# Starting the deferred normalisation of an attention group two key steps later, in a differential-attention layer on eight cores

## Chip, cores and metric

One Trainium2 chip, all 8 cores. Every core runs the same program on its own data. The metric is the device time in microseconds of the slowest core; "before" is the median of two runs.

## What is computed

One pre-norm transformer layer on x of shape (4, 4096, 1024): differential attention, then a gated two-expert feed-forward part. The change lies in the attention. Cut to what matters:

```python
# 16 heads, each with two score maps of depth 32 and values of width 64
scores = einsum('bhqd,bhkd->bhqk', q, k)            # 32 maps, s = 4096
probs  = softmax(scores, axis=-1).reshape(b, 16, 2, s, s)
w      = probs[:, :, 0] - lam * probs[:, :, 1]
attn   = einsum('bhqk,bhkd->bhqd', w, v)
rms    = rsqrt(mean(attn * attn, axis=-1) + 1e-5)
attn   = attn * rms * subln_g * (1 - LAMBDA_INIT)
```

Each core takes one batch element and half of its queries (2048), against all 4096 keys.

## The kernel before

The program has three parts: projections into SBUF (Kfm, Qfm, Vtm), the attention, and the output projection with the feed-forward part. Instructions are listed by hand per engine; each engine runs its list in order, and semaphores tie the lists together.

The attention is a loop over 64 groups (16 heads times 4 blocks of 512 queries, `n` at L650). Within a group the loop at L659 takes 32 key tiles of 128, `j`, called steps here. A step has:

- on TensorE (PE), L665 and L670: scores of tile j for the two maps, 32 rows deep, into psS (two halves, taken in turn);
- on PE, for tile j - 1, L678 and L683 (values, 64 columns each, into psA) and L688 and L692 (a matrix of ones, which gives the softmax sums, into psZ); they wait for the exponentials of tile j - 1;
- on ScalarE (ACT), L700: the exponentials of tile j, psS to pt, 128x1024.

L708 to L720 do the value and sum products of the last tile, behind the loop.

What is left of a group, its combine (`make_combine`, L593), is done during the next group. It is a list of 11 thunks:

- s1, VectorE (DVE), L599: reciprocal of psZ, 128x512; it waits until the group's last sum product is done
- s2, DVE, L603: psA times that, into tbuf
- s3, PE, L607: tbuf through Lmat (128x64, fp32), which forms the difference with lambda, into psZ
- s4 and s5, DVE, L611 and L615: copy to abuf, square to sqf
- s6, PE, L619: sqf through ones (64x64, fp32), the sum of squares, into psZ
- s7, DVE, L623: scale and epsilon; after it the psZ and psA of this group are free, which the group after next waits for in its first step (L663)
- s8 and s9, ACT, L629 and L633: Ln and Exp, which give the reciprocal root
- s10, DVE, L638: the scaled result to anbuf
- s11, POOL, L643 (issued in the helper at L108): DMA of anbuf to DRAM

Each fp32 product appears as two matmul instructions in the trace. Lines L704 and L705 put one thunk behind L700 of every even step from j = 4 on, so s1 stands at step 4, s3 at 8, s6 at 14, s8 at 18, s9 at 20 and s11 at 24. That a thunk stands at a step fixes its place in its own engine's list, and nothing else. What is left behind the loop would be issued at L724; the last group's combine is issued whole behind all groups (L727).

Of the kernel before, what the change touches and what calls it, by code (L numbers as in the profile page):

```python
# [63 lines left out]
def build_program(upto="full"):  # L64
# [46 lines left out]
    def T(fn, waits=(), inc=s_pe):  # L111
        return prog.op("tensor", fn, waits, inc)
# [4 lines left out]
    def A(fn, waits=(), inc=s_act):  # L117
        return prog.op("scalar", fn, waits, inc)
# [530 lines left out]
    pending = []  # L649
    for n in range(NGRP):  # L650
# [6 lines left out]
        if n >= 1:  # L657
            pending = make_combine(n - 1)
        for j in range(NT):  # L659
            p = j % 2  # L660
            waits = [(s_se, grp_exp_base + j - 1)]
            if j == 0:
                waits.append((s_dve, max(combine_free[n - 2], c_setup_done)))  # L663
                waits.append((s_act, c_p2_act))
            T(lambda t, p=p, r0=r0, g=g, j=j, qc=qc: t.matmul(  # L665
                psS[:, p * 1024: p * 1024 + 512],
                Kfm[r0:r0 + 32, g * S + j * 128: g * S + (j + 1) * 128],
                Qfm[r0:r0 + 32, g * QT + qc * 512: g * QT + (qc + 1) * 512],
                start=True, stop=True, tile_position=(r0, 0)), waits=waits)
            smm = T(lambda t, p=p, r1=r1, g=g, j=j, qc=qc: t.matmul(  # L670
                psS[:, p * 1024 + 512: p * 1024 + 1024],
                Kfm[r1:r1 + 32, g * S + j * 128: g * S + (j + 1) * 128],
                Qfm[r1:r1 + 32, g * QT + qc * 512: g * QT + (qc + 1) * 512],
                start=True, stop=True, tile_position=(r1, 0)), inc=s_smm)
            if j >= 1:
                jj = j - 1
                pm = jj % 2
                T(lambda t, jj=jj, pm=pm, d=d, aset=aset: t.matmul(  # L678
                    psA[aset][0:64, :], Vtm[:, jj * D + d * 64: jj * D + d * 64 + 64],
                    pt[:, pm * 1024: pm * 1024 + 512],  # L680
                    start=(jj == 0), stop=False, tile_position=(0, 0)),
                    waits=[(s_se, grp_exp_base + jj + 1)])
                T(lambda t, jj=jj, pm=pm, d=d, aset=aset: t.matmul(  # L683
                    psA[aset][64:128, :], Vtm[:, jj * D + d * 64: jj * D + d * 64 + 64],
                    pt[:, pm * 1024 + 512: pm * 1024 + 1024],
                    start=(jj == 0), stop=False, tile_position=(0, 64),
                    skip_group_check=True))
                T(lambda t, jj=jj, pm=pm, aset=aset: t.matmul(  # L688
                    psZ[aset][0:64, :], ones64b[:, :],
                    pt[:, pm * 1024: pm * 1024 + 512],  # L690
                    start=(jj == 0), stop=False, tile_position=(0, 0)))
                prog.op("tensor", lambda t, jj=jj, pm=pm, aset=aset: t.matmul(  # L692
                    psZ[aset][64:128, :], ones64b[:, :],
                    pt[:, pm * 1024 + 512: pm * 1024 + 1024],
                    start=(jj == 0), stop=False, tile_position=(0, 64),
                    skip_group_check=True), inc=s_satt)
            wexp = [(s_smm, smm)]
            if j >= 2:
                wexp.append((s_satt, s_satt.count - 1))
            A(lambda sc, p=p: sc.activation(pt[:, p * 1024: p * 1024 + 1024],  # L700
                                            psS[:, p * 1024: p * 1024 + 1024],
                                            AF.Exp, bias=mneg_bc[:, 0:1], scale=float(SCALE)),
              waits=wexp, inc=s_se)
            if pending and j >= 4 and (j % 2 == 0):  # L704
                pending.pop(0)()  # L705
        jj = NT - 1
        pm = jj % 2
# [454 lines left out]
```

How the kernel before makes its waits and increments, by code:

```python
    def replay(self, eng_obj, name):  # L54
        for ws, fn, inc, incn in self.items[name]:
            for (s, v) in ws:
                eng_obj.wait_ge(s.handle, v)
            instr = fn(eng_obj)
            if inc is not None:
                assert instr is not None, f"op on {name} must return an instruction"
                instr.then_inc(inc.handle, incn)
```

## Time and profile before

| | us |
|---|---|
| time, median of 2 runs | 4235.14 (4234.46 to 4235.81) |
| the profiled execution's own time | 4229.77 |
| its span (slowest core, core 7) | 4228.2 |
| spans of the other seven cores | 4182.9 to 4191.0 |
| PE busy (matmuls) | 3147.4, 74% |
| ACT busy | 2591.6, 61% |
| DVE busy | 1095.7, 26% |
| PE weight loads | 930.1, 22% |

Times below are microseconds from the start of the span unless they say ns. A row that names a line, an engine and an operation is one group of instructions; the arrow reads "out from in". "PEclk" is the share of TensorE's full clock that was granted in a stretch: 1.00 is 2.4 GHz, 0.50 is 1.2 GHz. An engine can be "busy" and still slow.

### The profile page before, as it was taken

The numbers are of one execution on the slowest core, as the hardware profiler recorded it, in microseconds if no ns is written. First come the engines' busy times: TensorE is split into PE (matmuls) and PEld (weight loads), VectorE is DVE, ScalarE is ACT, GpSimd is POOL, SyncE is SP. The second block draws the span as 40 slices with busy tenths as digits, with TensorE's granted clock in tenths as the row PEclk, the third lists the DMA queues.
The fourth block names the chain that finished last, engine by engine and source line by source line (L and its number), as shares of the span: only waits on it lengthen the run. The fifth ranks groups of instructions, "written<-read, shape, count | busy, mean of one in ns | idle before, by whom it ended". The sixth has DMA issues, their size and how long they took to land.

```text
span 4228.2 us, 48628 instructions; the slowest of 8 cores (4182.9 to 4228.2 us)
## 1 busy us (share of the span) xinstructions
PE 3147.4 (74%) x16100; PEld 930.1 (22%) x16100; DVE 1095.7 (26%) x2159; ACT 2591.6 (61%) x3590; POOL 71.1 (2%) x116
## 2 busy tenths in 40 slices
PE   2626637888788888888888878888888888715598
PEld 1313312222222222222222222111221222103332
DVE  3747735211111111111111111111111111116622
ACT  1424511478778778787787777777787777602211
POOL 0001100000000000000000000000000000000000
PEclk9868979789889889898898998776897788757799
DMA  2234421000000000000000000000000000023201
GB/s 82 77 105 119 122 74 45 18 2 2 3 2 3 2 2 3 2 3 2 2 3 2 2 3 2 2 2 2 2 3 2 2 2 3 2 84 93 65 35 45
DMA packets 96042, 108.20 MB, mean 26 GB/s; under 512 B 57780, under 2 KB 70198, under 8 KB 95800
## 3 DMA queue, kind: packets, MB, share of 16 engines
q1 hardware_dynamic: 88888, 84.11, 7.1%
q0 software_dynamic: 6912, 20.98, 1.7%
q8 instruction: 137, 2.24, 0.2%
q14 instruction: 105, 0.86, 0.1%
HBM read 84.09 MB, written 20.97 MB: 25 GB/s over the span
## 4 chain that ended last, share of the span: by engine, by line
PE 48%; ACT 25%; DMA 13%; issue 8%; DVE 4%; ACTq 1%; DVEq 0%; SPq 0%; POOL 0%; POOLq 0%
ACT pt L700 23%; PE psA L678 12%; PE psS L665 11%; PE psZ L688 8%; PE pp L292 4%; PE psE L1049 3%; PE psZ L607 2%; PE psE L1054 2%; DMA xbuf<-x 2%; PE psZ L619 2%; DMA stab<-sink 1%; PE psXO L855 1%; DMA ctab<-cosk 1%; DMA wst<-wo 1%; DMA xbuf<-xq 1%
## 5 line engine op out<-in xcount | busy, mean ns | idle before, releaser
L700 ACT ACTIVATE pt<-psS,mneg_bc 128x1024 bf16<-128x1024 f32 x2048 | 2198.6, 1110 | 642.8 <-PE psS L670 637.8
L678 PE MATMUL psA<-pt,Vtm 128*64 128x512 bf16 x1984 | 883.2, 445 | 456.0 <-ACT pt L700 419.3
L683 PE MATMUL psA<-pt,Vtm 128*64 128x512 bf16 x1984 | 921.4, 464 | 0.0
L692 PE MATMUL psZ<-pt,ones64b_s 128*64 128x512 bf16 x1984 | 885.8, 446 | 0.0
L688 PE MATMUL psZ<-pt,ones64b_s 128*64 128x512 bf16 x1984 | 883.2, 445 | 0.0
L665 PE MATMUL psS<-Qfm,Kfm 32*128 32x512 bf16 x2048 | 881.2, 435 | 1.2 <-DVE Lmat L561 1.2
L670 PE MATMUL psS<-Qfm,Kfm 32*128 32x512 bf16 x2048 | 881.8, 436 | 0.0
L678 PEld LDWEIGHTS psA<-pt,Vtm 128*64 128x64 bf16 x1984 | 221.5, 112 | 1076.7 <-issue 1076.7
L599 DVE RECIPROCAL zrbuf<-psZ 128x512 f32<-128x512 f32 x64 | 214.9, 3358 | 892.9 <-PE psZ L720 892.9
L665 PEld LDWEIGHTS psS<-Qfm,Kfm 32*128 32x128 bf16 x2048 | 184.4, 92 | 1097.4 <-issue 1097.4
L292 PE MATMUL pp<-wbuf,hfmb 128*128 128x512 bf16 x1280 | 334.8, 422 | 81.8 <-DMA hfmb<-hfm_s 42.2
L692 PEld LDWEIGHTS psZ<-pt,ones64b_s 128*64 128x64 bf16 x1984 | 239.3, 121 | 0.0
L688 PEld LDWEIGHTS psZ<-pt,ones64b_s 128*64 128x64 bf16 x1984 | 234.5, 118 | 0.0
L683 PEld LDWEIGHTS psA<-pt,Vtm 128*64 128x64 bf16 x1984 | 221.4, 112 | 0.0
L611 DVE COPY abuf<-psZ 64x512 f32<-64x512 f32 x64 | 43.7, 683 | 662.9 <-PE psZ L607 662.9
L292 PEld LDWEIGHTS pp<-wbuf,hfmb 128*128 128x128 bf16 x1280 | 130.2, 106 | 264.1 <-issue 158.5
L670 PEld LDWEIGHTS psS<-Qfm,Kfm 32*128 32x128 bf16 x2048 | 185.0, 93 | 0.0
L638 DVE TENSOR_TENSOR anbuf<-abuf,rstdb 64x512 bf16<-64x512 f32 x64 | 43.8, 684 | 474.0 <-ACT rstdb L633 474.0
L623 DVE TENSOR_SCALAR ubuf<-psZ 64x512 f32<-64x512 f32 x64 | 43.7, 683 | 428.9 <-PE psZ L619 428.9
L301 ACT CAST qef<-pp 128x512 bf16<-128x512 f32 x48 | 28.1, 585 | 185.5 <-DVE ropeo L314 180.1
L508 ACT CAST Vtm<-pp 128x512 bf16<-128x512 f32 x32 | 18.7, 585 | 192.7 <-PE pp L292 187.8
L855 PE MATMUL psXO<-wo_b,atile 128*128 128x512 bf16 x256 | 83.2, 497 | 70.3 <-DMA atile<-attn_s 70.0
(144 smaller groups left out, 2219.8 us busy)
## 6 DMA issues: line engine op xcount, KB each, us to landing
xbuf<-x SPq DMA_DIRECT2D x32, 512.0 KB
xbuf<-xq SPq DMA_DIRECT2D x16, 512.0 KB
hfm_s<-hfmb POOLq DMA_DIRECT2D x32, 256.0 KB, 3.2
hfmb<-hfm_s SPq DMA_DIRECT2D x32, 256.0 KB
xqb<-xq SPq DMA_DIRECT2D x16, 512.0 KB
wst<-w SPq DMA_DIRECT2D x32, 256.0 KB
out<-ybuf POOLq DMA_DIRECT2D x16, 512.0 KB, 3.0
ctab<-cosk SPq DMA_DIRECT2D x32, 128.0 KB
```

The costliest lines, as they stand in the source:

```text
L292: last = T(lambda t, n=n, c=c: t.matmul(pp[ppb][:, n * 512:(n + 1) * 512], hfm_tile[:, c * 128:(c + 1) * 128], wmat_b[:, c * D + n * 512: ...
L599: st["c1"] = V(lambda v: v.reciprocal(zrbuf[:, :], psZ[bset][:, :]), waits=[(s_satt, (m + 1) * NT)])
L607: st["c4"] = T(lambda t: t.matmul(psZ[bset][0:64, :], Lmat[:, :], tbuf[:, :], start=True, stop=True), waits=[(s_dve, st["c2"])])
L665: T(lambda t, p=p, r0=r0, g=g, j=j, qc=qc: t.matmul(psS[:, p * 1024: p * 1024 + 512], Kfm[r0:r0 + 32, g * S + j * 128: g * S + (j + 1) * 128],
L670: smm = T(lambda t, p=p, r1=r1, g=g, j=j, qc=qc: t.matmul(psS[:, p * 1024 + 512: p * 1024 + 1024], Kfm[r1:r1 + 32, g * S + j * 128: g * S ...
L678: T(lambda t, jj=jj, pm=pm, d=d, aset=aset: t.matmul(psA[aset][0:64, :], Vtm[:, jj * D + d * 64: jj * D + d * 64 + 64], pt[:, pm * 1024: p ...
L683: T(lambda t, jj=jj, pm=pm, d=d, aset=aset: t.matmul(psA[aset][64:128, :], Vtm[:, jj * D + d * 64: jj * D + d * 64 + 64], pt[:, pm * 1024 ...
L688: T(lambda t, jj=jj, pm=pm, aset=aset: t.matmul(psZ[aset][0:64, :], ones64b[:, :], pt[:, pm * 1024: pm * 1024 + 512], start=(jj == 0), sto ...
L692: prog.op("tensor", lambda t, jj=jj, pm=pm, aset=aset: t.matmul(psZ[aset][64:128, :], ones64b[:, :], pt[:, pm * 1024 + 512: pm * 1024 + 1024],
L700: A(lambda sc, p=p: sc.activation(pt[:, p * 1024: p * 1024 + 1024], psS[:, p * 1024: p * 1024 + 1024], AF.Exp, bias=mneg_bc[:, 0:1], scale ...
L855: mm = T(lambda t_, n=n, c=c, ab=ab: t_.matmul(psXO[:, n * 512:(n + 1) * 512], atile[ab][:, c * 128:(c + 1) * 128], wo_b[:, c * D + n * 51 ...
L1049: mm = T(lambda t_, n=n, c=c, t=t, wT=wT, e=e: t_.matmul(psE[e][:, n * 512:(n + 1) * 512], h2_all[:, t * D + c * 128: t * D + (c + 1) * 12 ...
```

## The change

The first step at which a thunk may be placed is 6 instead of 4. The thunks, their order, their waits and their number stay; s1 now stands at step 6, s3 at 10, s6 at 16, s8 at 20, s9 at 22 and s11 at 26.

```diff
@@ -701,7 +701,7 @@
                                             psS[:, p * 1024: p * 1024 + 1024],
                                             AF.Exp, bias=mneg_bc[:, 0:1], scale=float(SCALE)),
               waits=wexp, inc=s_se)
-            if pending and j >= 4 and (j % 2 == 0):
+            if pending and j >= 6 and (j % 2 == 0):
                 pending.pop(0)()
         jj = NT - 1
         pm = jj % 2
```

## Rows read from the trace of the kernel before

**Rows 1.** The page's costliest groups: busy us, mean ns, idle before and releaser.

```profile
L700 ACT ACTIVATE pt<-psS,mneg_bc 128x1024 bf16<-128x1024 f32 x2048 | 2198.6, 1110 | 642.8 <-PE psS L670 637.8
L678 PE MATMUL psA<-pt,Vtm 128*64 128x512 bf16 x1984 | 883.2, 445 | 456.0 <-ACT pt L700 419.3
```

**Rows 2.** The list of cores: span and mean granted clock.

```profile
core 0: 4183.5 us, clock 0.857
...
core 7: 4228.2 us, clock 0.838
```

**Rows 3.** Timeline of ACT, core 7: start, duration, instruction, idle before.

```profile
1520.45 1.11 ACT L700 ACTIVATE pt<-psS,mneg_bc 128x1024 bf16<-128x1024 f32 x1 [0.42 <-PE psS L670]
1521.98 1.11 ACT L700 ACTIVATE pt<-psS,mneg_bc 128x1024 bf16<-128x1024 f32 x1 [0.42 <-PE psS L670]
...
1530.36 2.12 ACT L700 ACTIVATE pt<-psS,mneg_bc 128x1024 bf16<-128x1024 f32 x2 [0.27 <-PE psS L670]
1532.74 2.12 ACT L700 ACTIVATE pt<-psS,mneg_bc 128x1024 bf16<-128x1024 f32 x2 [0.26 <-PE psS L670]
```

**Rows 4.** Table of stretches, core 7; the columns are its first line.

```profile
core 7: us, PE busy (x) PEld busy (x) DVE busy (x) ACT busy (x) POOL busy (x), PEclk, DMA share, GB/s
795.30:845.80 50.50, 49.12 (x194) 9.17 (x192) 0.57 (x1) 35.50 (x33) 0.00 (x0) 0.50 0.00 1
...
1517.07:1527.31 10.24, 10.18 (x36) 2.10 (x36) 0.23 (x1) 6.49 (x6) 0.00 (x0) 0.50 0.00 0
1527.31:1561.44 34.13, 25.76 (x161) 7.01 (x160) 6.35 (x6) 28.32 (x28) 0.53 (x1) 1.00 0.01 3
...
2643.40:2691.10 47.70, 46.15 (x172) 8.78 (x172) 6.78 (x6) 31.55 (x30) 0.53 (x1) 0.50 0.01 2
2895.94:2923.24 27.30, 25.89 (x101) 5.20 (x102) 4.05 (x2) 18.53 (x17) 0.00 (x0) 0.50 0.00 1
3049.60:3063.20 13.60, 13.49 (x50) 2.74 (x50) 2.56 (x2) 8.76 (x8) 0.00 (x0) 0.50 0.00 1
...
2874.89:2875.40 0.51, 0.51 (x3) 0.23 (x1) 0.00 (x0) 0.51 (x1) 0.00 (x0) 0.50 0.00 0
...
2970.85:2974.48 3.63, 3.63 (x12) 0.62 (x9) 1.37 (x2) 1.51 (x2) 0.00 (x0) 0.50 0.02 5
```

**Rows 5.** Timeline of PE, core 7, group 16: the seam and L607.

```profile
1514.75 0.38 PE L678 MATMUL psA<-pt,Vtm 128*64 128x512 bf16 x1 [1.17 <-ACT pt L700]
...
1525.65 1.82 PE L607 MATMUL psZ<-tbuf,Lmat 128*64 128x512 f32 x2
```

**Rows 6.** Stretches ahead of and behind L607, first and last of 63 each.

```profile
857.14:858.64 1.50, 1.50 (x9) 0.52 (x8) 0.00 (x0) 1.08 (x2) 0.00 (x0) 0.50 0.00 0
...
3651.01:3652.51 1.50, 1.50 (x9) 0.52 (x8) 0.00 (x0) 1.08 (x2) 0.00 (x0) 0.50 0.00 0
...
862.64:864.64 2.00, 1.77 (x12) 0.39 (x10) 0.00 (x0) 1.89 (x2) 0.00 (x0) 1.00 0.00 0
...
3656.51:3658.51 2.00, 1.50 (x11) 0.48 (x12) 0.00 (x0) 1.74 (x3) 0.00 (x0) 1.00 0.03 8
```

**Rows 7.** Timeline of PE, core 7, inside a long low stretch.

```profile
2644.54 1.97 PE L619 MATMUL psZ<-sqf,ones64f_s 64*64 64x512 f32 x2
```

**Rows 8.** Timeline of DVE, core 7: starts and ends of combines.

```profile
1513.15 3.36 DVE L599 RECIPROCAL zrbuf<-psZ 128x512 f32<-128x512 f32 x1 [12.94 <-PE psZ L720]
...
1544.10 0.68 DVE L638 TENSOR_TENSOR anbuf<-abuf,rstdb 64x512 bf16<-64x512 f32 x1 [7.69 <-ACT rstdb L633]
1557.72 3.36 DVE L599 RECIPROCAL zrbuf<-psZ 128x512 f32<-128x512 f32 x1 [12.94 <-PE psZ L720]
...
3048.12 3.36 DVE L599 RECIPROCAL zrbuf<-psZ 128x512 f32<-128x512 f32 x1 [12.94 <-PE psZ L720]
...
3093.38 3.36 DVE L599 RECIPROCAL zrbuf<-psZ 128x512 f32<-128x512 f32 x1 [12.94 <-PE psZ L720]
```

**Rows 9.** L607 by itself, core 7: ns min/median/max, what ended PE's idle time.

```profile
L607 PE MATMUL psZ<-tbuf,Lmat x128: 593/1061/1086, 858.6 to 3692.7; 128*64 128x512 f32 x128
its engine sat idle before it (us, times) until:
  issue: 33.1, 127
```

**Rows 10.** L599 by itself on core 0: ns min/median/max, first and last start.

```profile
L599 DVE RECIPROCAL zrbuf<-psZ x63: 3357/3358/3358, 837.9 to 3598.2; 128x512 f32<-128x512 f32 x63
```

## The prediction

> **What bounds the kernel now.** I read the page's costliest groups first. The exponentials of L700 are 2198.6 us of ACT and wait 637.8 us for scores, while L678 waits 419.3 us for exponentials [rows 1]. So the 64 attention groups, which begin at 795 us and are most of the span, are a ring of PE and ACT in which each waits for the other. Then the list of cores: core 7 is the slowest, 4228.2 us against 4183.5 on core 0, and its mean granted clock is lower, 0.838 against 0.857 [rows 2]. So PE's clock is worth following, and I did that inside single groups.
>
> A group has two paces. In the timeline of ACT for group 16, exponentials come 1.53 us apart at 1520.45, and in pairs 2.38 us apart at 1530.36, which is 1.19 us a step [rows 3]. The table of stretches says what goes with each pace: granted clock 0.50 (the 1.2 GHz level) from 1517.07 to 1527.31, and 1.00 (2.4 GHz) from 1527.31 to 1561.44 [rows 4]. In the slow stretch PE is full (10.18 of 10.24 us) and sets the pace; in the fast one it is busy 25.76 of 34.13 us and ACT sets it. A step costs 0.34 us more at the low clock.
>
> What PE did before the clock fell: it stood 1.17 us ahead of the first L678 of the group, at 1514.75, behind an exponential [rows 5]. Every group has this hole at its seam. What PE did before it rose: it ran the two fp32 passes of L607 (s3, Lmat times tbuf) from 1525.65 to 1527.47 [rows 5]. I asked the table for the 1.5 us ahead of L607 in the first 63 combines of core 7: 0.50 in each. Four to six us behind its start it is 1.00 in each [rows 6]. The distance from L607 to the rise runs from 0.5 us (2874.89 to 2875.40) to 3.6 us (2970.85 to 2974.48) [rows 4].
>
> Is L607 the cause, or only near it? Group 0 has no combine, and core 7 runs all of it, 50.50 us with PE busy 49.12, at 0.50. From 2643.40 to 2691.10 the clock stays at 0.50 for 47.70 us with PE busy 46.15 [rows 4], though L619 (s6) lies inside at 2644.54 [rows 7]. So in these rows the bf16 steps, which use 32 rows or 64 columns of the array, keep PE busy but do not lift the clock, nor does L619 with 64 rows. L607, with 128 rows, does.
>
> [...]
>
> **The change part by part.** Thunks fire at even steps from j = 6 instead of j = 4. There are 13 such steps up to 30 and 11 thunks, so s1 is at 6 and s11 at 26, and none falls into the drain after the loop. Nothing is added or removed. In the four queues:
>
> - DVE carries only combine work here. s1 (L599) starts at 1513.15, when L720 is done, and its place in the source puts nothing ahead of it [rows 8]. It is over at 1516.51 as before, and s2 behind it. Cost 0.
> - L607 on PE waits for s2, and runs 9.1 us after the end of s1, with no idle time of PE for DVE ahead of it [rows 5, 8, 9]. Two steps later there is only more slack. Its passes cost the same when the clock is low. L619 and the two activations L629, L633 stay 6, 10 and 12 steps behind L607. Behind L607 stand L665 and L670, and ACT waits for these; that hole moves but keeps its size.
> - The end of the chain is s10 (L638) at 1544.10, 13.6 us ahead of the next L599 at 1557.72, and s11's DMA behind it [rows 8]. Moved by two steps (2.4 to 3.1 us) it is still 10 us ahead. zrbuf, tbuf and abuf aren't late, and the psZ bank, released by L623 ahead of L638, is wanted only at the seam, over 13 us on. If this cover were gone, the first L665 of the next group would wait by what is missing. Cost 0.
> - The clock. With L607 two steps later, the stretch at 0.50 holds at least two more steps: 2 x 0.34 = 0.68 us a group, and 63 groups have it: 43 us. This is the lower bound if the cause is right.
> - The second part of the same term. Today the groups repeat: the fall comes 3.9 us after L599 starts (1513.15 to 1517.07), and L599 to L599 is 44.57 us (1513.15 to 1557.72) [rows 4, 8]. Where the clock was disturbed before, the fall sits elsewhere: in the group at 3048.12 it comes after 1.5 us, the low stretch is 13.60 us and the group 45.26 us (to 3093.38), 0.69 us more [rows 4, 8]. I expect that the new length breaks the repetition, so that the fall and the gap behind L607 wander over their spans. The upper bound is that every group pays this as well: 0.68 + 0.69 = 1.37 us, 86 us in all. I take the middle, 1.03 us or 65 us, since neither end has a reason to hold in all groups.
>
> Sum against the profiled execution: span 4228.2 + 1.6 around it = 4229.8, + 65 = 4295. Core 7 holds 45 us that the others don't (4228.2 against 4183.5), from stretches such as the 47.70 us at 0.50 [rows 2, 4]. If no core has as much in the runs to come, an undisturbed core gives 4185 + 65 = 4250. Both runs of before were at 4234 to 4236, which is 5 us above the profiled one, so some core had it each time, and I lower the sum by only 5: **4290**, 1.3% above the median of 4235.1. The case's own range is 4228 (undisturbed, lower bound: 4185 + 43) to 4321 (4235 + 86).
>
> **The rivals.**
>
> A, the forecast: L607 raises the clock, and it comes later. 62%.
>
> B, nothing moves: L607 is moved within slack and the clock's rise follows something that keeps its place, or the added low steps are taken from the hole at the seam. For it: no instruction gets a new wait. Against: the 63 rises behind L607 and none ahead of it. 4225 to 4245. 15%.
>
> C, mid-group falls spread. On core 7 the clock also falls in the middle of a group: 27.30 us at 0.50 from 2895.94 [rows 4]. After such a fall the group has no L607 left, so it stays low into the next one. Against the usual 10.24 us that is 17.1 us more at 0.50, and at 0.34 us in 1.53 it costs 3.8 us. If the wandering meets this in a third of the groups, that is 21 x 3.8 = 80 us more: 4370; in all of them about 4530. It passes 4320 from 8 such groups on. For it: these falls could be tied to where the clock's edges lie in a group, and that is what becomes loose. Against: core 0 has its L599 44.52 us apart in the mean (837.9 to 3598.2, 62 distances), so it had little of this [rows 10]. 14%.
>
> D, the other side: the clock rises by itself about 10 us after its fall (1517.07 to 1527.31 [rows 4]). Then L607, which would start about 12 us past the fall (8.6 now), meets 2.4 GHz. Its pass is 1061 ns in the median and 593 ns at the least [rows 9], so a pair saves 0.94 us, at most 63 x 0.94 = 59 us: 4171; with half of it hidden behind ACT, 4200. It decides if the rise comes before step 10. Against it: 49.12 us of busy PE at 0.50. 9%. [...]
>
> **How the numbers follow.** Predicted 4290 as A's likeliest. The range runs from 4228 to 4340: it holds A and most of B, and the lower part of C; D and the rest of C, together under 2 in 10, are left out. Two per cent, 85 us, is about what a measurement of this kernel tells from no change, so the bounds are 4150 and 4320. Slower by over 2%: most of C and a tail of A, 0.20. Faster by over 2%: 0.02, since even D's full saving stops at 1.5%. Within: 0.78.
>
> **What the profile after would show.** Right: L607 some 15.5 to 16.5 us after L599 starts (12.5 now), the clock 0.50 up to it and 1.00 soon behind; low stretches of 13.6 us and more; L599 to L599 45.2 to 46 us; the mean clock lower by about 0.02; L607, L619, L629 without waits. B: low stretches still 10.24 us, and L607 with passes of 593 ns would be D. C: low stretches over 27 us in many groups. Wrong in another way: a wait of L665 for DVE at the seam, or anything outside 795 to 3690 us that moves.

## The result, and the profile after

| | before | after |
|---|---|---|
| time, median | 4234.5 us (10 runs) | 4257.5 us (11 runs) |
| ratio after to before | | 1.0061, 95% interval 1.0041 to 1.0081 |
| profiled span, slowest core | 4228.2 | 4256.0 |
| profiled span, median of the eight cores | 4185.8 | 4246.6 |
| mean distance of two L599, all cores | 44.60 | 45.47 |

The change makes the kernel slower by 0.6%. Two numbers of this table pull apart: the slowest core lost 28 us, the median core 61 us. The list of cores of the changed kernel, to be read beside [rows 2]:

```profile
core 0: 4253.1 us, clock 0.814
...
core 3: 4224.8 us, clock 0.831
...
core 6: 4256.0 us, clock 0.815
core 7: 4243.3 us, clock 0.824
```

All eight cores now lie between 4225 and 4256 us with a clock of 0.812 to 0.831. Before, seven lay between 4183 and 4191, at 0.852 to 0.859, and one at 4228. No core is an exception any more. Groups with about 24 us or more at the clock of 0.50 were 8 in the trace before, 6 of them on core 7 and 2 on core 2; after the change there are 84, and each core has 5 to 14 of them (5 on core 3, the fastest).

The profile gives the clock as a granted share. On core 7 of the kernel before, products of L292 (512 columns) that follow each other start 216 ns apart at 1.00 and 427 ns apart at 0.50, in the median of 971 and 191 distances, which is 2.4 and 1.2 columns a ns. The 2.4 GHz and 1.2 GHz named ahead of this section are these rates at one column a clock, an estimate: no trace shows the frequency itself.

The page's two leading groups moved as the clock did (0.838 on the slowest core before, 0.815 after), beside [rows 1]: L678 takes 460 ns in the mean instead of 445, and ACT waits 24 us more for scores.

```profile
L700 ACT ACTIVATE pt<-psS,mneg_bc 128x1024 bf16<-128x1024 f32 x2048 | 2208.7, 1111 | 666.9 <-PE psS L670 661.8
L678 PE MATMUL psA<-pt,Vtm 128*64 128x512 bf16 x1984 | 913.3, 460 | 419.5 <-ACT pt L700 384.2
```

Inside a group of core 6, table of stretches (as [rows 4]) and timelines of PE and DVE:

```profile
core 6: us, PE busy (x) PEld busy (x) DVE busy (x) ACT busy (x) POOL busy (x), PEclk, DMA share, GB/s
2486.80:2503.90 17.10, 16.62 (x62) 3.35 (x62) 2.93 (x2) 11.37 (x11) 0.00 (x0) 0.50 0.00 0
2503.90:2614.30 110.40, 85.30 (x528) 23.39 (x526) 16.68 (x17) 93.00 (x92) 1.59 (x3) 1.00 0.01 3
...
2650.80:2678.10 27.30, 25.89 (x101) 5.13 (x101) 4.05 (x2) 18.45 (x17) 0.00 (x0) 0.50 0.00 1
```

```profile
2501.93 1.92 PE L607 MATMUL psZ<-tbuf,Lmat 128*64 128x512 f32 x2
2504.15 0.40 PE L678 MATMUL psA<-pt,Vtm 128*64 128x512 bf16 x1
```

```profile
2485.68 3.36 DVE L599 RECIPROCAL zrbuf<-psZ 128x512 f32<-128x512 f32 x1 [10.56 <-PE psZ L720]
2531.51 3.36 DVE L599 RECIPROCAL zrbuf<-psZ 128x512 f32<-128x512 f32 x1 [10.56 <-PE psZ L720]
2572.72 3.36 DVE L599 RECIPROCAL zrbuf<-psZ 128x512 f32<-128x512 f32 x1 [10.56 <-PE psZ L720]
2613.91 3.36 DVE L599 RECIPROCAL zrbuf<-psZ 128x512 f32<-128x512 f32 x1 [10.56 <-PE psZ L720]
```

Three things are to be seen. The clock falls 1.1 us after L599 at 2485.68 and rises only 2.0 us behind L607, which starts 16.3 us after L599 (12.5 before): 17.1 us at 0.50 instead of 10.24, and the group is 45.83 us long instead of 44.57 [rows 8]. Second, the next two groups have no low stretch at all and take 41.2 us each; I hadn't foreseen that. Third, a mid-group fall as on core 7 before now lies here on core 6, 27.3 us from 2650.80.

Groups 1 to 62 of all eight cores, 496 of them, by their time at 0.50, counted from the granted clock in the two traces (a group here runs from its first exponential to that of the next):

| at 0.50 in the group | before: groups, mean length | after: groups, mean length |
|---|---|---|
| under 4 us | 0 | 81, 41.6 us |
| about 10 us | 417, 44.37 us | 2, 44.2 us |
| about 14 us | 47, 45.40 us | 96, 45.25 us |
| about 17 us | 24, 45.33 us | 124, 45.85 us |
| about 20 us | 0 | 109, 46.13 us |
| about 24 us and more | 8, 49.3 us | 84, 48.1 us |

The one repeating kind of group is gone, and the new ones lie on both sides of it. In the mean of these groups the time at 0.50 grew from 11.2 to 16.1 us. In both traces every rise in these groups (496 before, 413 after) comes 0.5 to 3.9 us behind the start of L607.

### The profile page after: what moved, and what is told of

It is laid out like the page before. It is cut to its first block, busy times and chain, and to the rows that moved or that the text cites. A ratio compares the mean times of both kernels' runs of the same rounds, so it can differ in the third digit from the quotient of the medians.

```text
span 4256.0 us, 48628 instructions; the slowest of 8 cores (4224.8 to 4256.0 us)
## 1 busy us (share of the span) xinstructions
PE 3217.3 (76%) x16100; PEld 932.1 (22%) x16100; DVE 1094.1 (26%) x2159; ACT 2601.9 (61%) x3590; POOL 71.3 (2%) x116
## 4 chain that ended last, share of the span: by engine, by line
PE 50%; ACT 23%; DMA 15%; issue 8%; DVE 3%; ACTq 1%; SPq 0%; DVEq 0%; POOL 0%; POOLq 0%
ACT pt L700 21%; PE psA L678 13%; PE psS L665 12%; PE psZ L688 8%; PE pp L292 3%; PE psE L1049 3%; DMA xbuf<-x 3%; PE psZ L607 2%; DMA stab<-sink 2%; PE psE L1054 2%; DMA ctab<-cosk 2%; PE psZ L619 2%; PE psXO L855 1%; DMA xbuf<-xq 1%; DMA wst<-wo 1%
## 5 line engine op out<-in xcount | busy, mean ns | idle before, releaser
L678 PE MATMUL psA<-pt,Vtm 128*64 128x512 bf16 x1984 | 913.3, 460 | 419.5 <-ACT pt L700 384.2
L683 PE MATMUL psA<-pt,Vtm 128*64 128x512 bf16 x1984 | 948.2, 478 | 0.0
L665 PE MATMUL psS<-Qfm,Kfm 32*128 32x512 bf16 x2048 | 917.0, 453 | 1.2 <-DVE Lmat L561 1.2
L670 PE MATMUL psS<-Qfm,Kfm 32*128 32x512 bf16 x2048 | 917.1, 453 | 0.0
L692 PE MATMUL psZ<-pt,ones64b_s 128*64 128x512 bf16 x1984 | 914.9, 461 | 0.0
L688 PE MATMUL psZ<-pt,ones64b_s 128*64 128x512 bf16 x1984 | 912.8, 460 | 0.0
L678 PEld LDWEIGHTS psA<-pt,Vtm 128*64 128x64 bf16 x1984 | 223.9, 113 | 1069.5 <-issue 1069.5
L599 DVE RECIPROCAL zrbuf<-psZ 128x512 f32<-128x512 f32 x64 | 214.9, 3358 | 755.9 <-PE psZ L720 755.9
L292 PE MATMUL pp<-wbuf,hfmb 128*128 128x512 bf16 x1280 | 332.7, 419 | 82.2 <-DMA hfmb<-hfm_s 43.5
L611 DVE COPY abuf<-psZ 64x512 f32<-64x512 f32 x64 | 43.7, 683 | 835.5 <-PE psZ L607 835.5
L692 PEld LDWEIGHTS psZ<-pt,ones64b_s 128*64 128x64 bf16 x1984 | 244.7, 123 | 0.0
L688 PEld LDWEIGHTS psZ<-pt,ones64b_s 128*64 128x64 bf16 x1984 | 240.0, 121 | 0.0
L292 PEld LDWEIGHTS pp<-wbuf,hfmb 128*128 128x128 bf16 x1280 | 129.7, 106 | 263.2 <-issue 156.1
```

The source lines that it names most:

```text
L292: last = T(lambda t, n=n, c=c: t.matmul(pp[ppb][:, n * 512:(n + 1) * 512], hfm_tile[:, c * 128:(c + 1) * 128], wmat_b[:, c * D + n * 512: ...
L599: st["c1"] = V(lambda v: v.reciprocal(zrbuf[:, :], psZ[bset][:, :]), waits=[(s_satt, (m + 1) * NT)])
L665: T(lambda t, p=p, r0=r0, g=g, j=j, qc=qc: t.matmul(psS[:, p * 1024: p * 1024 + 512], Kfm[r0:r0 + 32, g * S + j * 128: g * S + (j + 1) * 128],
L670: smm = T(lambda t, p=p, r1=r1, g=g, j=j, qc=qc: t.matmul(psS[:, p * 1024 + 512: p * 1024 + 1024], Kfm[r1:r1 + 32, g * S + j * 128: g * S ...
L678: T(lambda t, jj=jj, pm=pm, d=d, aset=aset: t.matmul(psA[aset][0:64, :], Vtm[:, jj * D + d * 64: jj * D + d * 64 + 64], pt[:, pm * 1024: p ...
L683: T(lambda t, jj=jj, pm=pm, d=d, aset=aset: t.matmul(psA[aset][64:128, :], Vtm[:, jj * D + d * 64: jj * D + d * 64 + 64], pt[:, pm * 1024 ...
```

## The experiments

Each time is compared with runs of the kernel before on the same chip. Those gave 4222.9, 4219.2, 4208.9 and 4222.2 us in the four series, so the ratios are what to compare. The expected times of the first two series were written from 4235 us for the kernel before, so a time in its range can still be 12 to 16 us off as a difference. "Median core" is the median span of the eight cores in the timed runs: 4187 to 4193 us for the kernel before in these series, 4240 us for the changed one.

### Only L607 moved, and only L607 moved back

`e1_s3_late`, on the kernel before (s3 at step 10, with s4; all of PE, ACT and POOL else as it was):

```diff
-            if pending and j >= 4 and (j % 2 == 0):
+            if j in (4, 6, 10, 14, 16, 18, 20, 22, 24) and pending:
+                pending.pop(0)()
+            if j in (10, 12) and pending:
                 pending.pop(0)()
```

> The kernel before with L607 (s3) at step 10 instead of 8 and every other combine instruction of PE, ACT and POOL at its old step (s6 at 14, s8 at 18, s9 at 20, s11 at 24). Theory 'L607 lifts the clock': the low stretches grow as in the changed kernel, most 13.6 us or longer, group length 45.3 to 45.6 us in the mean of the cores, time 4245 to 4270. Rival 'one of the other moved instructions does it': low stretches stay at 10.24 us and the time at 4235.

Measured: 4285.2 us, ratio 1.0147 (1.0110 to 1.0184); median core 4250, which is 58 us above the kernel before beside it. Mean distance of two groups 45.6 us, 70 groups with under 4 us at 0.50, the others 14 us or more. The low stretches are those of the changed kernel:

```profile
1124.75:1141.75 17.00, 16.67 (x62) 3.35 (x62) 2.79 (x2) 11.22 (x11) 0.00 (x0) 0.50 0.00 0
```

The slowest core was worse than I expected (4279 to 4293 in the four runs, for 4245 to 4270), since core 1 had the lowest mean clock in each run, 0.799 to 0.804. The median core says what matters: L607 alone makes a loss as large as that of the whole change.

`e2_s3_back`, on the changed kernel:

```diff
-            if pending and j >= 6 and (j % 2 == 0):
+            if j in (4, 6, 8, 12, 14, 16, 18, 20, 22, 24, 26) and pending:
                 pending.pop(0)()
```

> The changed kernel with L607 back at step 8 and everything else of the combine at its new step (s6 at 16, s8 at 20, s9 at 22, s11 at 26). Theory 'L607': low stretches 10.24 us again, groups 44.4 us, time 4230 to 4240. Rival 'another moved instruction': as the changed kernel, 4250 to 4260.

Measured: 4235.9 us, ratio 1.0038 (1.0012 to 1.0063), median core 4212. With L607 back at step 8 the repetition is back too: 342 of 496 groups with about 10 us at 0.50, 44.37 us each, none without a low stretch. Core 0:

```profile
1109.10:1119.25 10.15, 10.15 (x36) 2.07 (x36) 0.17 (x1) 6.42 (x6) 0.00 (x0) 0.50 0.00 0
1119.40:1153.40 34.00, 25.68 (x161) 7.01 (x160) 6.56 (x6) 28.54 (x29) 0.53 (x1) 1.00 0.01 3
```

The time hits the range, but beside its own runs of the kernel before (4222.9) it is 13 us more. What is left, some 20 us on the median core, goes with more mid-group falls (41 groups with about 24 us or more at 0.50, 8 before), so the later s6 to s9 seem to take a share. Moved alone, L607 costs 58 us; the rest alone 20; all together about 50. The parts don't add up, and how the loss divides was not shown.

### Does L607 lift the clock? The same product with 128 and with 64 rows

`e4_twice128` issues s3 once more at step 6 in the changed kernel, `e5_twice64` the same on half of the rows:

```diff
+        def s3x():
+            T(lambda t: t.matmul(psZ[bset][0:64, :], Lmat[0:128, :], tbuf[0:128, :],
+                                 start=True, stop=True), waits=[(s_dve, st["c2"])])
...
-        return [s1, s2, s3, s4, s5, s6, s7, s8, s9, s10, s11]
+        return [s1, s2, s3x, s3, s4, s5, s6, s7, s8, s9, s10, s11]
...
+            if j == 6 and pending:
+                pending.pop(0)()
+                pending.pop(0)()
+                pending.pop(0)()
-            if pending and j >= 6 and (j % 2 == 0):
+            if pending and j >= 10 and (j % 2 == 0):
                 pending.pop(0)()
```

(`e5_twice64` has `Lmat[0:64, :], tbuf[0:64, :]`.)

> The changed kernel with s3 issued twice, once at step 6 and once at step 10, same operands and same target; the first result is overwritten by the second, so nothing of the computation changes. Added work: two fp32 passes a group, 1.6 us of PE in a stretch in which PE is the bound. Theory 'L607 lifts the clock': it rises 0.5 to 3.9 us after the copy at step 6, 9 to 10 us after L599 starts; low stretches 6.8 to 10.2 us; the real s3 then runs at 2.4 GHz and saves 0.9 us, the steps 6 to 10 save 1.4 us. Mean group about 44.8 us, time 4200 to 4240, not above the changed kernel although work is added. Rival 'the clock rises when step 10 is reached or by itself': the copy only costs, 63 x 1.6 = 100 us more, 4350.

> As e4_twice128, but the copy at step 6 takes only rows 0 to 63 of Lmat and tbuf; its result is overwritten as well. Same free size, same type, same place, half the rows of the array. Theory 'rows of the array count': the clock doesn't rise behind the copy but behind the real s3 at step 10; group 47 us, time 4340 to 4370. Rival 'any fp32 product lifts it' (or any stretch of PE without a wait): as e4_twice128, 4200 to 4240.

Measured: 4314.1 us (1.0210, 1.0170 to 1.0251) with 128 rows, 4500.3 us (1.0648, 1.0598 to 1.0699) with 64. Timeline of PE, then table of stretches, with 128 rows (core 4); L611 is the copy at step 6, L607 the real s3:

```profile
1828.95 1.65 PE L611 MATMUL psZ<-tbuf,Lmat 128*64 128x512 f32 x2
1835.18 1.02 PE L607 MATMUL psZ<-tbuf,Lmat 128*64 128x512 f32 x2
```

```profile
1823.40:1830.25 6.85, 6.75 (x24) 1.55 (x24) 0.27 (x1) 4.30 (x4) 0.00 (x0) 0.50 0.00 0
1830.25:1864.30 34.05, 26.70 (x163) 7.25 (x162) 3.22 (x5) 27.50 (x28) 0.53 (x1) 1.00 0.01 3
```

The same two views with 64 rows (core 0):

```profile
1083.21 1.97 PE L611 MATMUL psZ<-tbuf,Lmat 64*64 64x512 f32 x2
1091.10 1.92 PE L607 MATMUL psZ<-tbuf,Lmat 128*64 128x512 f32 x2
```

```profile
1074.15:1094.55 20.40, 20.00 (x70) 3.91 (x70) 4.18 (x4) 12.11 (x12) 0.00 (x0) 0.50 0.00 1
1094.70:1096.70 2.00, 1.50 (x12) 0.43 (x10) 0.00 (x0) 1.76 (x3) 0.00 (x0) 1.00 0.00 0
```

The 128-row copy ends the low stretch 1.3 us behind its start. The 64-row copy, in the same place and no shorter, doesn't: the clock waits for the real L607, which starts 7.9 us later. Over all cores, 495 of 503 rises come 0.6 to 3.8 us behind the start of the 128-row copy, and all 469 rises of the other kernel 0.5 to 3.9 us behind the real L607. So between these two fp32 products the rows decide. At step 6 neither the place in the group, nor PE busy 20.00 of 20.40 us, nor fp32 as such made the rise. That is shown, with the time in the balance: 186 us between two kernels that differ in rows alone. It doesn't say that 128 rows are enough. The value and sum products of each step (L678 to L692) have 128 rows by 64 columns too, in bf16, and the clock didn't rise behind them in the 50.50 us of group 0 [rows 4].

My sizes were off for both. `e4_twice128` was to be 4200 to 4240: 390 low stretches last 6.8 or 10.2 us as expected, but in 72 groups the clock fell again some 20 us into the group and stayed low until the next copy, and such a group takes 51.9 us. `e5_twice64` was to be 4340 to 4370; its groups are 48.7 us in the mean, since the low stretches came out at 17 to 20 us, and in some 170 of 496 groups a mid-group fall came on top.

### L607 two steps earlier than before

`e3_from2`: `j >= 2` in place of `j >= 4` in the kernel before, L607 at step 6.

> The kernel before with the combine started at step 2 instead of 4, so L607 stands at step 6 instead of 8. Theory 'L607 lifts the clock': it rises about 3 us earlier; the short low stretches are 6.8 us instead of 10.24, groups 43.6 us where nothing else falls, that is 50 us less: 4170 to 4190. Against it stands what the run with s3 twice showed: with the clock up early, 72 of some 490 falls came in mid-group, 20 us after the group began, and such a group takes 52 us; if that comes back in one group of seven, it eats 60 us and the time is 4220 to 4250. Rival 'position of L607 doesn't matter': 4235.

Measured: 4226.8 us, ratio 1.0018 (0.9991 to 1.0045), no difference; the median core is 10 us slower, 4200 us against 4191, with 54 groups at about 24 us or more at 0.50 where before had 8. The time lies in the range that I tied to the mid-group falls, but the short low stretches on which both sums rest are not there. In 383 of 496 groups the low stretch is 10.24 us as before and the group 44.34 us. Core 0, timeline of DVE and table of stretches:

```profile
1103.36 3.36 DVE L599 RECIPROCAL zrbuf<-psZ 128x512 f32<-128x512 f32 x1 [15.33 <-PE psZ L720]
1147.72 3.36 DVE L599 RECIPROCAL zrbuf<-psZ 128x512 f32<-128x512 f32 x1 [15.33 <-PE psZ L720]
```

```profile
1104.95:1115.05 10.10, 10.10 (x36) 2.08 (x36) 2.46 (x2) 6.44 (x6) 0.00 (x0) 0.50 0.00 0
1115.20:1149.20 34.00, 25.75 (x161) 7.01 (x160) 4.21 (x5) 28.47 (x29) 0.53 (x1) 1.00 0.01 3
```

The fall simply comes earlier in the group, 1.6 us after L599 instead of 3.9. Whole cycles of 10.2 us low and 34.1 us high, 44.36 us from L599 to L599, repeat in these 383 groups: L607 two steps earlier shifts the cycle against the group and leaves its length. L607 two steps later breaks it. Of the 4.9 us more at 0.50 in a group of the changed kernel, two slow steps of 1.53 us would make 3.1. How its loss divides between them and the lost repetition was not isolated, nor why the repetition holds with L607 at step 6 and 8 and not at 10. A low stretch of about 14 us goes with a group of 45.25 us in the table above, which is 0.9 us longer than the cycle.

### What makes the clock fall

`e6_seam` puts the last products of a group (L708 to L720) behind the first scores of the next one, and with them the wait for the banks to the first value product; `e7_fill` leaves the order and fills the hole with five bf16 products of 128 rows and 128 columns. Of the first edit only the place of the products is shown.

```diff
+            if j == 0 and last is not None:
+                last_products(*last, grp_exp_base)
...
```

```diff
+            if j == 1:
+                for _ in range(5):
+                    T(lambda t, aset=aset: t.matmul(
+                        psA[aset][:, :], Vtm[:, 0:128], Kfm[:, 0:512],
+                        start=True, stop=True))
```

> The kernel before with the seam of two groups closed: the last value and sum products of a group are issued behind the first scores of the next one, and the wait for the psZ and psA bank goes to the first value product. No work added or left out; L607 stays at step 8. Theory 'the hole of PE at the seam makes the clock fall': no fall at the seam, most groups at 2.4 GHz throughout, 39.5 to 41.5 us each (41.2 was a group without a low stretch in the changed kernel, less the 1.2 us hole): 3930 to 4060. Rival 'the clock falls anyway, whatever the seam': only the hole of about 1.2 to 1.9 us a group is gone, 4115 to 4160.

> The kernel before with five extra bf16 products of 128 rows by 128 columns by 512 in the hole of PE at the seam, into psA ahead of its first real product, which overwrites them. ACT's wait at the seam stays. Theory 'the hole makes the clock fall': the added products take the fall away from the seam, most groups 41 to 42 us, 4040 to 4120. Rival 'the fall has another cause': low stretches of 10.24 us stay, and the products add up to 5 x 0.38 us less the 1.17 us hole, 0 to 0.7 us a group: 4235 to 4280.

Measured: `e6_seam` 4147.7 us (0.9824, 0.9789 to 0.9858), `e7_fill` 4136.1 us (0.9800, 0.9760 to 0.9840). Core 0 of `e6_seam`, two groups and what follows:

```profile
1280.90:1361.40 80.50, 63.75 (x392) 17.69 (x392) 13.56 (x12) 70.48 (x69) 1.06 (x2) 1.00 0.01 3
1361.40:1384.80 23.40, 18.66 (x112) 5.15 (x112) 6.10 (x5) 19.60 (x20) 0.00 (x0) 1.00 0.00 0
1384.95:1422.35 37.40, 37.37 (x142) 7.32 (x144) 5.42 (x4) 26.37 (x26) 0.53 (x1) 0.50 0.01 3
```

In the trace before, PE stands 0.96 to 1.45 us at each of the 504 seams, and 465 of 488 falls come in the first 5 us of a group. Without the hole 156 of 158 falls come in mid-group and the other two 3.0 us into a group; 221 of 496 groups run wholly at 1.00, 40.3 us each. But the clock falls in mid-group, here 23.5 us into the third, where PE is busy 80% with the ordinary steps, and stays low 37.4 us. So in this kernel the fall at the seam, 465 times before and twice here, comes from the hole; it isn't the only cause of a fall, and my sum, which took the others for rare, was 90 us too low. The time lies in the range of the rival, for which only the hole would be gone, and on that side the rival was right: a group has 11.5 us at 0.50 in the mean, no less than before (11.2). The falls moved, and the gain is about what the hole took: a group without a low stretch takes 1.15 us less than in `e12_before_fill` below, which has the hole, so 63 of them make 73 us; 72 were measured on the slowest core and 83 on the median core. In `e7_fill`, 16 us above its range, 227 groups have next to no low stretch, 41.3 us each; the others have mid-group falls or the tail of one. The time at 0.50 is 7.7 us a group, since a low stretch ends behind the next five products, in 153 of 158 cases 1.2 to 4.0 us behind their start. So in this kernel the rise came behind bf16 products too. Group 0, which has no combine and was low for 50.50 us [rows 4], rises behind the five products of step 1.

```profile
797.40:801.90 4.50, 4.50 (x17) 1.05 (x15) 0.00 (x0) 2.33 (x3) 0.00 (x0) 0.50 0.00 0
802.10:838.50 36.40, 28.61 (x184) 7.93 (x182) 0.30 (x1) 32.99 (x30) 0.00 (x0) 1.00 0.00 1
```

### Keeping the clock up

On `e6_seam`, one product of 128 rows by 128 columns in each step (`e8_each`), in each second step (`e9_second`), or five at four steps (`e10_burst`), into the psA bank that s2 has read. The edit of `e9_second`, without the line in s2 that sets `free_psA`:

```diff
+            if j >= 7 and j % 2 == 1:
+                c2w = [(s_dve, free_psA[0])] if n else []
+                T(lambda t, aset=aset: t.matmul(
+                    psA[1 - aset][:, :], Vtm[:, 0:128], Kfm[:, 0:512],
+                    start=True, stop=True), waits=c2w)
```

> e6_seam with one extra bf16 product of 128 rows by 128 columns by 512 in every step from step 7 on, in all groups, into the psA bank that lies idle (its content was read by s2 and is overwritten by the next group). 25 products a group, 0.22 us each at 2.4 GHz, partly in the 0.44 us that PE waits every second step. Theory 'the bf16 steps fill few rows or columns, and that is why the clock falls in mid-group and does not come back by itself': nearly no low stretch, group 0 too at 2.4 GHz, groups 40.3 to 42.5 us, 3990 to 4110 against about 4145 of e6_seam. Rival 'only PE idle time counts, or the fillers cost as much as they give': low stretches in mid-group stay and each filler costs 0.2 to 0.4 us, 45 us a group, 4250 or more.

> As e8_each, but in every second step (13 products a group). Theory as there: fewer low stretches than e6_seam (163 in some 490 groups there), groups 41 to 42.5 us, 4020 to 4110; dearer than e8_each if the dose is too low, cheaper if the fillers of e8_each are on the path. Rival: 4145 to 4200.

> As e8_each, but five products in one go at steps 7, 15, 23 and 31. The five at the seam in e7_fill lifted the clock within the group's first 4 us. Theory: falls in mid-group remain but a low stretch ends behind the next burst, at most 8 steps on (12 us) instead of 15 to 48 us; a burst of 1.1 us costs some 0.6 us beyond the idle time it fills, 2.4 us a group; groups 42.5 to 43.5 us, 4080 to 4160. Rival 'a burst doesn't lift it away from the seam': 4145 + 63 x 2.4 = 4300.

Measured: `e8_each` 3958.8 us (0.9400, 0.9386 to 0.9414), `e9_second` 3952.5 us (0.9398, 0.9374 to 0.9422), `e10_burst` 4184.5 us (0.9950, 0.9931 to 0.9970). Core 4 of `e9_second`:

```profile
795.00:845.00 50.00, 48.12 (x179) 9.35 (x181) 0.00 (x0) 31.27 (x29) 0.00 (x0) 0.50 0.00 1
900.00:3300.00 2400.00, 2040.78 (x12150) 580.28 (x12357) 401.53 (x356) 2132.73 (x2011) 31.12 (x59) 1.00 0.01 3
```

The clock stays at 1.00 for 2400 us, ACT is busy 89% of them, and the eight cores lie within 17 us of each other (3934.5 to 3951.1). 482 groups of 496 have no low stretch and take 40.54 us; those of `e8_each` take 40.73, so the 12 further products of a group cost 0.19 us. This beats both kernels, by 6% or more. The times lie below my ranges (3990 to 4110 and 4020 to 4110). One thing in these rows went against my words: in every second step, single products kept the clock up for those 2400 us, but didn't lift it: the 14 rises behind group 0 come 0.4 to 3.4 us behind the start of L607. Group 0 stays at 0.50 in `e9_second` for its whole length, 56.06 us on each of the eight cores, although it has 13 of them. In every step they did lift: in `e8_each` the clock rises inside group 0 on all eight cores, 14 to 39 us after its first exponential. Core 0 of `e8_each`:

```profile
783.90:801.95 18.05, 17.11 (x64) 3.22 (x62) 0.00 (x0) 12.13 (x11) 0.00 (x0) 0.50 0.00 0
802.10:827.70 25.60, 25.50 (x151) 7.02 (x149) 0.00 (x0) 23.39 (x21) 0.00 (x0) 1.00 0.01 2
```

The bursts did lift (134 low stretches, none longer than 10.3 us, each over at most 2.8 us behind the start of a product of a burst), but a group without a low stretch takes 43.4 us with them, 3.1 us more than in `e6_seam`, and that eats the gain; I had put 2.4 us on it, and the time is 25 us above its range.

`e12_before_fill` has the products of `e9_second` and the seam of the kernel before.

> The kernel before, seam as it was, with the extra product of every second step from step 7 on alone. It parts what the seam gives from what the products give. Theory 'the hole at the seam makes the clock fall, the products stop the mid-group falls and lift it behind a seam fall': the fall at the seam stays in many groups and the clock rises behind the first product at step 7 or soon after, before L607; group 0 rises too; groups 42 to 44 us, 4070 to 4170. Rival 'the products alone keep the clock up': 41.4 to 41.6 us a group, 4000 to 4020.

Measured: 4164.7 us, ratio 0.9870 (0.9846 to 0.9894). Core 0, a group without and one with a fall at the seam:

```profile
1023.30:1064.70 41.40, 34.50 (x208) 9.73 (x209) 6.79 (x7) 35.83 (x34) 0.53 (x1) 1.00 0.01 2
1241.35:1251.35 10.00, 9.30 (x37) 2.23 (x37) 0.69 (x1) 6.96 (x7) 0.00 (x0) 0.50 0.00 0
```

Falls in mid-group are gone but for one. The fall at the seam stays in two groups of three, and such a low stretch lasts until L607 (340 rises, 0.2 to 3.6 us behind its start). I had expected the first single product, at step 7, to lift the clock, and group 0 to rise too; the one didn't, and group 0 is at 0.50 to its last microsecond, so the time lies in my range (4070 to 4170) by luck.

Cores 6 and 7 have a third level in three groups each: from about 1193 us to 1343 and 1340 us the clock behind L607 is 0.81 and not 1.00, and these groups take 46.7 to 47.8 us. The low stretches between are as everywhere else. Why it was granted there wasn't tested. Core 6:

```profile
1200.02:1213.67 13.65, 13.11 (x49) 2.70 (x46) 2.34 (x4) 8.49 (x8) 0.00 (x0) 0.50 0.00 0
1213.67:1247.81 34.14, 30.77 (x163) 7.60 (x163) 4.39 (x4) 27.51 (x28) 0.53 (x1) 0.81 0.01 3
```

So the cures take different losses: the seam alone gives 1.8%, and by the counts above that is the hole itself; the products alone give 1.3%, by ending the mid-group falls; with both, 482 of 496 groups have no low stretch, and the gain is 6.0%.

### The studied change once more, with the clock held up

`e11_second_s3late` is `e9_second` with L607 at step 10, s6 at 16, s8 at 20 and s11 at 26, as the changed kernel has them.

```diff
-            if pending and j >= 4 and (j % 2 == 0):
+            if pending and j == 6:
+                pending.pop(0)()
+                pending.pop(0)()
+            if pending and j >= 10 and (j % 2 == 0):
                 pending.pop(0)()
```

> e9_second with the combine's products and activations where the changed kernel has them (L607 at step 10, s6 at 16, s8 at 20, s11 at 26). With the clock at 2.4 GHz nearly throughout, the position of L607 can act only through the instruction queues. Theory 'position acted through the clock alone': as e9_second, 3950 to 3965, at most 5 us apart. Rival 'two steps later also costs in the queues': the 20 to 60 us of the studied change come back, 3975 to 4010.

Measured: 3954.6 us (0.9367, 0.9351 to 0.9383), in the range of the first theory; 485 groups without a low stretch, 40.55 us each, against 40.54 in `e9_second`. With the clock up the two steps cost nothing in any queue (2 us between the two kernels). So the effect of the change goes through PE's clock, as far as this kernel, with its closed seam, stands for the one before.

## Why the prediction was right in direction and wrong in size

**The direct part, cost 0: right.** `e11_second_s3late` shows it without the clock. In the changed kernel L607 has no wait for DVE either, but for one of 4.4 us in the last group's combine, which the kernel before has too, and L599 starts when L720 is done.

**The cause, L607 lifts the clock: right.** `e1_s3_late` and `e2_s3_back` single L607 out of what moved, and `e4_twice128` against `e5_twice64` shows that it is the product itself. Rivals B and D fall: the low stretches grew, and where the clock had fallen it did not rise ahead of L607 (413 rises, 0.5 to 3.9 us behind its start). The prediction's words for the reason, "32 rows or 64 columns of the array", are not right as they stand: L607 itself is 128 rows by 64 columns [rows 5], the shape of the value and sum products, behind which it did not rise in the 50.50 us of group 0. What sets L607 apart from those (fp32, or two passes on end) was not tested.

**The size of a group's loss: near, for a partly wrong reason.** I had 0.68 us for two slow steps and half of 0.69 for the broken repetition, 1.03 us a group and 65 us. Measured are 0.87 us in the mean of all cores (44.60 to 45.47), 55 us over 63 groups; the median core of the timed runs lies at 4240 us against 4186 in the profile before. The sum hides two things that nearly cancel. Long low stretches, my rival C, came true in 84 groups of 496 (8 before). By C's own price, 3.8 us each, ten and a half such groups a core are worth 40 us. And 81 groups, ten a core, have next to no low stretch. They take 41.6 us, 3.8 us less than the 45.4 that I forecast, which is 39 us a core the other way, and no step of mine allowed them. I had asked how much later the rise comes, and took it for granted that the fall comes in each group.

**The step that failed: adding this term to the slowest core.** "Both runs of before were at 4234 to 4236 [...] so some core had it each time, and I lower the sum by only 5." The 65 us went on top of a core that already held 42 us more than the median core, in disturbed groups. But that surplus was made of the same thing that the change spreads over all cores (6 of the 8 groups with long low stretches lay on core 7; afterwards each core has 5 to 14), and it did not stay on top. In the profiles, the slowest core lies 42 us above the median core before and 9 us after; in the timed runs after it is 10 us in the median, in 13 runs of the kernel before in the first series, on another chip, 33 us. Three of the eleven timed runs after still have 25 to 36 us, so the surplus is rarer and not gone. So a median core 50 to 60 us slower shows as 23 us in the time of the slowest. The case that I named for it, an undisturbed core plus 65 us, gives 4250, and 4257 was measured. I held it to be the less likely one because I counted the disturbance as a property of the run and not as the same wandering that I forecast for every group.

**The repetition.** I took its break for a side effect worth half of 0.69 us. `e3_from2` speaks for a larger part: L607 two steps earlier leaves the time the same (0.2% slower on the median core), two steps later costs 1.2% on the median core. A cost per step, which would give a gain on one side and a loss on the other, is refuted.

**Open.** What starts a fall in mid-group, where PE is busy 80% with ordinary steps, was not isolated; that it all but goes with one product of 128 rows by 128 columns in every second step was shown (two falls later than 5 us into a group in `e9_second`, 156 in `e6_seam`). Why 81 of 496 groups in the changed kernel pass the seam without a low stretch was not tested.

## What to carry to other kernels

Where a trace shows two levels of PE's clock inside a loop, as 0.50 and 1.00 here, look in single iterations for what runs ahead of each rise and what is missing ahead of each fall. In this kernel each of the 496 rises came 0.5 to 3.9 us behind L607, an instruction "with slack", and two steps of delay to it alone cost 58 us on the median core (`e1_s3_late`). The products of this kernel's steps (32 rows by 128 columns, or 128 by 64, in bf16) kept PE busy for 49.12 of 50.50 us in group 0 without a rise, and with the seam closed the clock still fell 156 times in mid-group (`e6_seam`). Products of 128 rows by 128 columns in every second step, and no hole where two groups meet, were together worth 6.0% here (`e9_second`). For a time that is the slowest of eight cores, forecast the median core and the spread apart, and ask whether the change moves the surplus of the slowest or only spreads it.

## What the runs showed of the hardware that I had not expected

- 50.5 us of full PE at 0.50 without a rise [rows 4], and the rise behind a 128-row product where the 64-row one of equal length (1.9 us at the low clock) has none. The busy share in the profile (49.12 of 50.50 us) did not decide here.
- Five bf16 products of 128 rows by 128 columns together lifted the clock (group 0 of `e7_fill`, after 3.6 to 4.9 us); thirteen single ones spread over a group didn't (group 0 of `e9_second`, 56.06 us at 0.50), but they kept it up once it was there (2400 us); 25 of them, one in each step from 7 on, lifted it after 14 to 39 us (group 0 of `e8_each`).
- A cycle of 10.2 us low and 34.1 us high repeated with the group of 44.36 us in two kernels with L607 at different steps (417 groups of 496 in the kernel before, 383 in `e3_from2`).
- A third granted level, 0.81, on two cores of one die for three groups each of `e12_before_fill`, beside PE busy 30.77 of 34.14 us; on all eight cores of `e9_second` nothing of it was seen in the groups.
